# Sixty-four full pairs and seven 128-row border blocks in place of 71 padded pairs of an MoE layer's expert rows

## What is computed

```python
probs = jax.nn.sigmoid(logits)
scores, indices = jax.lax.top_k(probs, TOP_K)            # TOP_K = 2 of 8
scores = scores / jnp.sum(scores, axis=-1, keepdims=True)
w = w.at[jnp.arange(t)[:, None], idx].add(sc)
g = jax.nn.silu(jnp.einsum('th,ehi->tei', xf, gate_w))   # h = 256, i = 512
u = jnp.einsum('th,ehi->tei', xf, up_w)
combined = jnp.einsum('tei,eih,te->th', g * u, down_w, w)
return shared + combined.reshape(b, s, h)
```

## Time and profile before

| | us |
|---|---|
| median of three runs | 1612.41 |
| the profiled execution, its own time | 1612.66 |
| its span, first to last instruction | 1611.1 |
| PE busy | 1582.4 (98% of the span) |
| DVE busy | 1188.3 (74%) |
| ACT busy | 997.8 (62%) |
| POOL busy | 547.9 (34%) |

### The profile page before, as it was taken

The page is one execution under the profiler, slowest core; times in us unless marked ns, Lnnn a source line. Parts: engine busy times, 40 slices in busy tenths (PEclk is TensorE's granted clock), DMA queues, the critical chain, the costliest instruction groups (busy, mean ns, idle before and its releaser), DMA issues.

```text
span 1611.1 us, 37339 instructions
## 1 busy us (share of the span) xinstructions
PE 1582.4 (98%) x12578; PEld 1524.2 (95%) x12579; DVE 1188.3 (74%) x2444; ACT 997.8 (62%) x1735; POOL 547.9 (34%) x607
## 2 busy tenths in 40 slices
PE   8999999999999999999999999999999999999998
PEld 7799999999999998999999999999999999999997
DVE  6677787778777787888776666666666666666587
ACT  5566666666665656666655666666666666666653
POOL 2546645332300001477761222222222222222231
PEclk9999999999999999999999999999999999999999
DMA  4233343421101325432243132133123231111697
GB/s 126 85 121 125 128 139 122 139 79 46 40 27 34 138 112 166 152 120 97 100 151 96 61 104 63 58 110 112 56 92 105 82 111 58 60 56 50 182 299 187
DMA packets 72298, 168.75 MB, mean 105 GB/s; under 512 B 13188, under 2 KB 18692, under 8 KB 71560
## 3 DMA queue, kind: packets, MB, share of 16 engines
q1 hardware_dynamic: 47560, 102.35, 18.8%
q0 software_dynamic: 23248, 62.97, 13.2%
q10 hardware_dynamic: 1392, 2.10, 0.4%
HBM read 95.99 MB, written 71.39 MB: 104 GB/s over the span
## 4 chain that ended last, share of the span: by engine, by line
PE 51%; POOL 4%; DVE 2%; issue 2%; DMA 2%; ACT 0%; POOLq 0%; DVEq 0%; ACTq 0%; SPq 0%
PE f_bank L981 31%; PE f_bank L32 5%; PE f_bank L34 5%; PE f_bank L33 5%; POOL x_rows L1453 4%; PE f_bank L963 2%; PE f_bank L954 1%; DMA y_rows<-more_rows,goes_to 1%; DMA w_all<-y_rows 1%; DVE Z L1974 1%; DVE w_all L1967 1%; PE f_bank L1630 0%; PE f_bank L1632 0%; DVE f_prod L1036 0%; PE f_bank L1647 0%
## 5 line engine op out<-in xcount | busy, mean ns | idle before, releaser
L981 PE MATMUL f_bank<-xT_hi,w_cur_hi 128*128 128x256 f32 x1136 | 321.6, 283 | 0.9 <-ACT f_silu_g L1016 0.9
L981 PE MATMUL f_bank<-xT_hi,w_cur_lo 128*128 128x256 f32 x1136 | 321.5, 283 | 0.0
L981 PE MATMUL f_bank<-xT_lo,w_cur_hi 128*128 128x256 f32 x1136 | 321.5, 283 | 0.0
L1471 POOL DMA_INDIRECT y_rows<-more_rows,goes_to x142 | 138.9, 978 | 439.3 <-ACT more_rows L1574 252.5
L1036 DVE TENSOR_TENSOR f_prod<-f_silu_g,f_bank 128x512 f32<-128x512 f32 x206 | 141.6, 687 | 111.9 <-PE f_bank L981 109.3
L1959 DVE TENSOR_TENSOR w_cur_lo<-w_all,w_cur_hi 128x1024 fp32r<-128x1024 f32 x142 | 173.5, 1222 | 63.4 <-ACT w_cur_hi L1541 63.3
L981 PEld LDWEIGHTS f_bank<-xT_hi,w_cur_hi 128*128 128x128 f32 x1136 | 217.8, 192 | 1.0 <-issue 1.0
L981 PEld LDWEIGHTS f_bank<-xT_hi,w_cur_lo 128*128 128x128 f32 x1136 | 218.1, 192 | 0.0
L981 PEld LDWEIGHTS f_bank<-xT_lo,w_cur_hi 128*128 128x128 f32 x1136 | 217.9, 192 | 0.0
L981 PE MATMUL f_bank<-xT_hi,w_shared 128*128 128x256 f32 x1024 | 202.7, 286 | 0.5 <-PEq L58 0.5
L441 ACT ACTIVATE prob<-s_pair,negmax 128x1024 f32<-128x1024 f32 x128 | 142.1, 1114 | 89.5 <-DVE negmax L794 89.5
(11 more groups left out here) (304 smaller groups left out, 4389.5 us busy)
## 6 DMA issues: line engine op xcount, KB each, us to landing
more_rows<-x_rows POOLq DMA_DIRECT2D x71, 260.0 KB, 3.0
XS<-in_x SPq DMA_DIRECT2D x32, 256.0 KB, 3.1
XR<-in_x SPq DMA_DIRECT2D x32, 256.0 KB, 2.9
x<-XR SPq DMA_DIRECT2D x32, 256.0 KB, 2.2
Z<-x SPq DMA_DIRECT2D x4, 2048.0 KB, 12.2
w_all<-y_rows SPq DMA_DIRECT2D x32, 256.0 KB, 6.9
w_all<-y_rows POOLq DMA_DIRECT2D x32, 256.0 KB, 7.2
out<-Z SPq DMA_DIRECT2D x31, 256.0 KB, 5.9
```

The costliest lines, as they stand in the source:

```text
L981: mm = pe.matmul(out[:, 2 * P * i:2 * P * i + 2 * P], w, x, start=(c == 0 and n == 0), stop=(c == HC - 1 and n == 2))
L1471: pool.indirect_dma_start(d.y_rows, bass.IndirectOffsetOnAxis(ap=goes_to[:, par, t:t + 1], axis=0), y[:, t, :], None).then_inc(y_sent[t], 16)
```

## The change

The 16384 rows, expert after expert, are thought of as one line without padding. 64 pairs of tiles cut the line into pieces of 256 rows, and each pair is computed with the weights of the expert at its middle row. Where a border between two experts does not fall on a pair's middle, up to 128 rows of the neighbour stand in the wrong pair; one border block of 128 rows for each of the seven borders computes these rows with the neighbour's weights. So there are still 71 steps, 64 of two tiles and 7 of one (`short`, `tiles_of`): step 10 i + 4 is the block of border i.

- **PE**: in a short step the gate and up matmuls have 128 moving columns instead of 256 (their count stays 48), two transposes instead of four, 12 down matmuls instead of 24.
- **Loop** (`pairs`): steps 0 to 9 and 60 to 70 are written out; the loop runs i = 1 to 5 over a body of ten steps.
- **Border weights**: ACT (`load_border`, at steps 10 i + 1) loads the border's expert's gate and up weights (two DMAs of 512 KB) and down weights (1 MB) into `w_shared`. At step 66 ACT loads the shared weights back (`load_shared`, 2 MB and 1 MB); PE waits for that after step 70.
- **Plan** (DVE): 48 operations instead of 27; the last three move from behind step 38's product to behind step 39's.
- **SP** takes its next expert from the plan (`turn_expert`), since an expert may have no pair of its own; each expert's down weights lie in a tensor of their own (`down_parts`). The rows of padding are written by eight DMAs instead of one.
- **POOL** loads 128 rows for a short step, and for its missing second tile writes one row with a plain DMA that keeps the semaphore's count.

```diff
                     x_hi, x_lo = flat(xT_hi, c), flat(xT_lo, c)
                     w_hi, w_lo = hi(c)[:, o:o + P], lo(c)[:, o:o + P]
                     for n, (w, x) in enumerate(((w_hi, x_hi), (w_hi, x_lo), (w_lo, x_hi))):
-                        mm = pe.matmul(out[:, 2 * P * i:2 * P * i + 2 * P], w, x, start=(c == 0 and n == 0),
+                        mm = pe.matmul(out[:, 2 * P * i:2 * P * i + tiles * P], w, x, start=(c == 0 and n == 0),
                                        stop=(c == HC - 1 and n == 2))
...
@@ -1292,24 +1305,33 @@
 
         def pairs(eng, step):
 
-            for j in range(4):
-                step(j, j % 2)
-            with eng.Fori(2, NP // 2 - 1) as i:
-                step(2 * i, 0)
-                step(2 * i + 1, 1)
-            for j in range(NP // 2 * 2 - 2, NP):
-                step(j, j % 2)
-
-        def experts(eng, j):
-
-
-            at_pack = at(j // 2 if isinstance(j, int) else half(j, 0))
-            packed = eng.value_load(d.table[0:1, 1, at_pack], min_val=0, max_val=E ** 4 - 1)
+            for j in range(TURN):
+                step(j, j, 0)
+            with eng.Fori(1, BORDERS - 1) as i:
+                for r in range(TURN):
+                    step(TURN * i + r, r, i)
+            for j in range(TURN * (BORDERS - 1), NP):
+                step(j, j % TURN, j // TURN)
+
+        def short(r):
+
+            return r % TURN == BORDER_AT
+
+        def tiles_of(r):
+
+            return 1 if short(r) else 2
+
...
-                if e >= 2:
-
-                    end = sp.value_load(d.ends_i[0:1, e - 2:e - 1], min_val=0, max_val=2 * NP)
+            for turn in range(1, E):
+                e = sp.value_load(d.turn_expert[0:1, turn:turn + 1], min_val=0, max_val=E - 1)
+                if turn >= 2:
+                    end = sp.value_load(d.ends_i[0:1, turn - 2:turn - 1], min_val=0, max_val=2 * NP)
                     hold(sp, d, f.y_mm, end + ALL)
                 for k in range(PIECES):
-                    load_weights(e, k, PIECE)
-                    sp.wait_ge(d.w_ready, 16 * (PIECES * (e - 1) + k + 1) + 64)
+                    load_weights(turn, e, k, PIECE)
+                    sp.wait_ge(d.w_ready, 16 * (PIECES * (turn - 1) + k + 1) + 64)
 
...
-            def load(j, par):
+            def load(j, par, tiles):
                 row = pool.value_load(d.table[0:1, 0, at(j)], min_val=0, max_val=d.all_rows - 2 * P)
-                pool.dma_start(h[:, par, :, :], d.x_rows[ds(row, 2 * P), :].rearrange("(p t) h -> p t h", t=2)
+                pool.dma_start(h[:, par, 0:tiles, :], d.x_rows[ds(row, tiles * P), :].rearrange("(p t) h -> p t h", t=tiles)
                                ).then_inc(h_in[par], 16)
 
-            def scatter(j, par):
+            def scatter(j, par, tiles):
                 for t in range(2):
                     if t == 1 or inside(j - 1, NP):
                         hold(pool, d, y_sent[1 - t], 16 * j + 16 * t)
+                    if t == tiles:
+
+                        pool.dma_start(d.y_rows[2 * T:2 * T + 1, :], d.pad[0:1, 0:H]).then_inc(y_sent[t], 16)
+                        continue
                     hold(pool, d, y_copied, 2 * j + t + 1)
                     pool.indirect_dma_start(d.y_rows, bass.IndirectOffsetOnAxis(ap=goes_to[:, par, t:t + 1], axis=0),
                                             y[:, t, :], None).then_inc(y_sent[t], 16)
 
-            def step(j, par):
+            def step(j, r, i):
+                par = r % 2
...
 
-            def split_high(j, n, e):
+            def load_border(i):
+
+                after = ALL if isinstance(i, int) and i == 0 else 2 * TURN * i + (ALL + 2 * (BORDER_AT + 1 - TURN))
+                act.wait_ge(f.y_mm, after)
+                e = act.value_load(d.border_expert[0:1, at(i)], min_val=0, max_val=E - 1)
+                for part in range(2):
+                    act.dma_start(d.border_raw[:, W * part:W * part + W],
+                                  d.raw[part][ds(e, 1)].rearrange("o p n -> p (o n)")).then_inc(border_ready, 16)
+                act.dma_start(d.border_down[:].bitcast(F32),
+                              d.down_parts[ds(e, 1)].rearrange("o p a n -> p (o a n)")).then_inc(border_ready, 16)
+
+            def load_shared():
+
+                act.wait_ge(f.y_mm, ALL + 2 * (TURN * (BORDERS - 1) + BORDER_AT + 1))
+                both = d.w_shared[:].rearrange("p (a n) -> p a n", a=2)
+                act.dma_start(both[:, :, 0:2 * W].bitcast(F32), d.w_parts[0, :, :, 0:2 * W]).then_inc(d.shared_ready, 16)
+                i = 2 + ALL // TB
+                act.dma_start(both[:, :, 2 * W:3 * W].bitcast(F32), d.w_parts[i // 3, :, :, W * (i % 3):W * (i % 3) + W]
+                              ).then_inc(d.shared_ready, 16)
+
+            def split_high(j, n, e, i=None):
 
...
 
             who = []
 
-            def step(j, par):
+            def step(j, r, i):
+                par = r % 2
                 if par == 0:
-                    who[:] = experts(act, j)
+                    who[:] = experts(act, r, i)
+                if r == 1 and not (isinstance(i, int) and i == BORDERS):
+                    load_border(i)
+                if isinstance(j, int) and j == TURN * (BORDERS - 1) + BORDER_AT + 2:
...
             who = []
 
-            def step(j, par):
+            def step(j, r, i):
+                par = r % 2
                 if par == 0:
-                    who[:] = experts(pe, j)
+                    who[:] = experts(pe, r, i)
                 last = isinstance(j, int) and j == NP - 1
                 for n in range(2):
                     m, k = place_of(j, par, n)
                     if last:
                         turn(L0 + n)
                     elif n == 1:
-                        turn_two(j + 1, 1 - par)
+                        turn_two(j + 1, 1 - par, tiles_of(r + 1))
                     if n == 1:
                         if inside(j - 1, NP):
-                            down_two(j - 1, 1 - par, who[par])
+                            down_two(j - 1, 1 - par, who[par], tiles_of(r - 1))
                         else:
                             down_pair(ALL - 2)
                     pe.wait_ge(w_lo_done, 2 * j + n + 1)
-                    f.pe_pair_gate_up(pe, m, k, current, f.prod_done, m - 1)
+                    f.pe_pair_gate_up(pe, m, k, current, f.prod_done, m - 1, tiles=tiles_of(r))
 
             pairs(pe, step)
+            pe.wait_ge(d.shared_ready, 80)
             for i in range(LATE):
                 m = L0 + i
...
                 dve.wait_ge(sent[PLAN_GROUP % RING], ONCE * (PLAN_GROUP // RING + 1))
                 op(dve.tensor_tensor(count[:], base[:, GROUPS, :], d.first_row[:, 0:E], ALU.subtract))
-                op(dve.tensor_tensor(over, count[:].unsqueeze(2).to_broadcast([P, E, d.most]),
-                                     c.limits[:].unsqueeze(1).to_broadcast([P, E, d.most]), ALU.is_gt))
-                op(dve.tensor_reduce(nblocks[:], over, AX_X, ALU.add))
 
...
-                op(dve.tensor_copy(ends[:], nblocks[:]))
+                op(dve.tensor_copy(ends[:], count[:]))
                 for e in range(1, E):
-                    op(dve.tensor_tensor(ends[:, e:e + 1], ends[:, e - 1:e], nblocks[:, e:e + 1], ALU.add))
+                    op(dve.tensor_tensor(ends[:, e:e + 1], ends[:, e - 1:e], count[:, e:e + 1], ALU.add))
 
             def plan_starts():
                 op(dve.memset(starts[:, 0:1], 0.0))
...
-                op(dve.scalar_tensor_tensor(out=moved[:], in0=starts[:], scalar=-2.0 * P, in1=d.first_row[:, 0:E + 1],
+                op(dve.scalar_tensor_tensor(out=moved[:], in0=starts[:], scalar=-1.0, in1=d.first_row[:, 0:E + 1],
                                             op0=ALU.mult, op1=ALU.add))
                 op(dve.tensor_tensor(jump[:], moved[:, 1:E + 1], moved[:, 0:E], ALU.subtract))
...
+            def plan_borders():
...
+                log_p = P.bit_length() - 1
...
+                op(dve.tensor_scalar(side_i[:], ends_of_borders[:], log_p, 1, ALU.logical_shift_right, ALU.bitwise_and))
+                op(dve.tensor_copy(block_f[:], block_of[:]))
...
+                op(dve.tensor_copy(d.border_expert[:], side[0:1]))
+                op(dve.scalar_tensor_tensor(out=of_borders(c.own_rows)[:, :, 0], in0=block_f[:], scalar=float(P),
+                                            in1=c.row_of[:], op0=ALU.mult, op1=ALU.add))
+
+            def plan_turns():
...
+                op(dve.tensor_scalar(last_slot[:], behind_end[0:1], -1.0, float(NP), ALU.mult, ALU.add))
+                op(dve.memset(present[:, 0:1], 0.0))
...
+                op(dve.tensor_reduce(last_of_turn[:], square_1, AX_X, ALU.max))
+                op(dve.tensor_scalar(d.ends_i[:], last_of_turn[:], 2.0, None, ALU.mult))
+                op(dve.tensor_tensor(square_1, down(numbers), across(turn_of[:]), ALU.is_gt))
+                op(dve.tensor_reduce(of_turn[:], square_1, AX_X, ALU.add))
...
```

(29 more changed lines are left out.)

194 lines of the change are left out of this document (128 added, 66 removed).

## The result

The changed kernel takes 1628.04 us (three runs, 1627.11 to 1628.10) against 1612.41: ratio 1.0108 (95% interval 1.0093 to 1.0122), 15.6 us slower. The forecast was 1612.0 us, no change. The profiled execution has a span of 1626.5 us against 1611.1, 15.4 more, and the trace says where they are.

The account below looks back on a forecast made before the run. PE's instruction issue was taken to bound the expert steps (busy 634.88 of 636 us). Terms -13.9 + 2.8 + 2.7 + 8.0 = -0.4 us on the profiled 1612.66, 0.25 above the median, gave 1612.0 us, range 1601 to 1620.

Parts of the forecast that it names:

- Term 1: PE in the seven short steps: fewer columns, down matmuls and transposes save 1.98 us each, 13.9 us gained.
- Term 2: Step behind a border block: DVE's product comes late and PE stalls for `aT_lo`, 0.4 x 7 = 2.8 us (0 to 8.7).
- outside of everything: Signs the prediction would not cover: a drop of the granted clock in the stage, or PE waits on `w_cur_lo`.
- Term 3: The plan ends later, so PE's wait for the first pair grows from 2.3 to 5.0 us: +2.7 us.
- Term 4: Jump back of the ten-step loop: PE refetches its body and idles 2.0 us, four times: +8.0 us (0 to 13.6).
- DVE, ACT and POOL stop beside it: At the loop's turn the other engines turn behind PE and would stop beside it; nothing added for them.
- The rival of the border weights' traffic: Bursts of border loads make POOL's scatters land late, 2.5 us each, 20 us in all; half gives 1622; chance 0.12.
- The long body stays resident: Rival: the ten-step loop body is not fetched again, term 4 is 0 and the time is 1604 us; chance 0.28.

Follow-up runs that it names:

- The new order behind a border block: The marked version with the weights' parts put first on ACT and DVE in the step behind a border block: 1606.24 us, ratio 0.9969.
- The plan's new order: The marked version with the first-row table finished earlier, POOL waiting for 29 operations, and parts of the plan ahead of products: 1605.54 us, ratio 0.9967.
- the written-out version: The changed kernel with all 71 steps written out and no loop: 1609.05 us, ratio 0.9983 to the kernel before.
- the marked version: The changed kernel with a mark at the loop's head that names the jump back ahead of time: 1609.74 us, ratio 0.9992 to the kernel before.
- the best: The marked version with the plan and border-block steps reordered, border weights in six pieces and shared weights over three steps: 1598.94 us, ratio 0.9920.

## Why the prediction was wrong

Each term beside what it came to, in us against the kernel before:

| | foretold | measured | from |
|---|---|---|---|
| 1 short steps | -13.9 | -14.4 | 7 x 2.05 |
| 2 late work behind them | +2.8 | +6.4 | 2 x 0.59, 5 x 1.04 |
| 3 the plan | +2.7 | +6.1 | the later start, 4.15, and the clock's 1.95 |
| 4 the loop's turn | +8.0 | +15.8 | column 0 |
| late scatters | a rival | +3.7 | column 2 |
| ordinary steps, one long step of before, the end | 0 | -2.1 | the rest |
| sum | -0.4 | +15.5 | |

The span's own difference is 15.4. Late scatters were 0 in the sum and a rival beside it.

- **Term 1 held.** 128 columns against 256 save 0.008 us a matmul: they start 0.11 us apart in the short step too (897.58, 897.69, 897.80 in the trace). By the Trainium skill's 81 ns for a matmul with its weight load at 128 columns (TensorE: Matmul & The Clock Gate, Back-to-back issue gap) I estimate another 1.5 us saved in each short step; the trace, with 0.11 us, does not have it.
- **Term 2 named the wrong wait.** I followed the product to `aT_lo` and gave 0.4 us. PE does not wait for `aT_lo`; it waits one half earlier, for `w_cur_lo`, which I had put outside of everything. Outside the loop it costs 0.59 us a border, near my price. In the loop it is 1.04, and the loop itself makes the difference: written out, column 6 is 8.23 to 8.24 us in steps 10 to 59 too, where the loop has 8.69. What in the loop does it is read from the trace and not tried alone: between ACT's output and the next `w_cur_hi` its sequencer computes addresses that change with the loop, and the second starts 0.76 us behind the first (994.48 and 995.24 us) instead of 0.39 (905.12 and 905.51). The new order behind a border block removed nearly all of the wait, which shows the place.
- **Term 3 was right in its wait and blind behind it.** From 2.3 to 4.9 us was foretold as 2.3 to 5.0. Missed were the clock, 1.95 us in the first step (11.08 against 9.13 before), and 1.5 us ahead of it, where the 21 new operations that I spread over idle time stood in front of `f_aT_lo` (waits of 2.4 us in all against 0.2). I had bounded those at 2 us more and taken nothing. The 1.5 is known only roughly: with the plan of before the stage began anywhere from 840.8 to 843.3 us in five kernels. The plan's new order undid both.
- **Term 4 is the step that failed.** The mechanism was the forecast one, at the forecast places, with q8 packets where there were none. The size was half: I took a stop of 3.0 us less a lead of 1.0 and got 2.0 us a turn; measured is 3.14 us of idle PE and 0.8 us for the clock. The branch shows which half of the subtraction was wrong. It takes 4.05 us on average, 3.83 beyond its usual 0.22, which is over my upper bound of 3.4, built from one landing of a DMA and a packet's own time. The lead that was left to hide it is 3.83 - 3.14 = 0.69 us, not far from 1.0. How those 3.83 us divide between fetches and waiting is open. The clock's fall had no place in the sum, though I had named it as something outside of it. "DVE, ACT and POOL stop beside it" holds for DVE in this kernel, but not as nothing: with PE's body short, DVE's stops cost 10.5 us (8.1 of them as waits of PE in the profile).
- **The rival of the border weights' traffic** was real with a small price: five steps longer, 3.7 us in all in place of 10, with scatters of up to 7.8 us, over my threshold of 4.4, that cost 0.4 to 1.6 us each. In the written-out version one scatter took 8.99 us and its step was 4.65 us longer, more than the 2.5 that I had named for one.
- **The long body stays resident** was refuted as the code stood, and is what the mark brings about. The Trainium skill's sentence that a taken branch outside the window held waits for a fetch (Runtime: NRT & Kernel Launch, Instruction fetch mechanics) agrees with the trace: 4.05 us for the branch, with q8 packets around it. The Trainium skill's sizes, 2048 instructions on PE and 512 on others, do not agree by themselves: some 1500 instructions on PE were fetched again each turn, and DVE's 375 stopped at each.

That the measured time lies 8 us above the range has the same reasons: it ended at 1620 because term 4's bound held no clock and the terms' upper ends were never all taken together. Here every cost went past its value, and only the gain of term 1 came out as it should.

## What to carry to other kernels

Compare the instructions of a loop's body on each engine with a fetch packet before making it longer: here eight steps (4.9 packets on PE) were free, ten cost 4 to 5 us at each jump back, and a mark at the head took it all away. Price an idle time of TensorE of 2 us or more with the slow matmuls that can follow it, 1.1 to 2.4 us where they came, and not with its length alone. When a step is made shorter, look for every operand that was just in time in it, the weights as well as the activations; an edit of a few lines that moves these ahead took the ratio from 0.9992 to 0.9969, nearly a third of the way from the marked version to the best.

## What was not expected of the hardware

- The clock falls after short stops, and not after each. Start to start, stops of 2.56 us (before, at the first pair), 2.57, 2.62, 3.08 and 3.39 us had no slow matmuls behind them; 2.14, 2.65, 2.89 and 3.69 us had 12 to 16; of two stops of 2.64 us in different kernels one had them and one did not; the waits of 5.1 to 5.3 us for the first pair all had. What decides between them is open.
- The mark kept all 6.1 packets resident instead of fetching them earlier: no q8 packet between 1016 and 1391 us in the changed kernel, and none between 1117 and 1502 us in the kernel before with ten steps.
- Behind a marked loop, four steps on, a stop can follow: step 63 had one of 1.9 to 2.6 us in the profiles of six of the eight runs of marked versions of the changed kernel. In the best one DVE stands still from 1403.7 to 1406.4 us between two register instructions, with no jump there, and a q14 packet came at 1404.7. The written-out version has no such stop; the cause was not tried.
- Each DMA issue by ACT, with the read of its table entry, took 0.8 to 1.1 us of its sequencer, of which the issue alone was mostly 0.34 to 0.40; single issues took 1.44 and 2.07 us.
